# Second step of a graph layer: the rows of the second hop shifted by one product, and adjacency chunks issued among the feature reloads

## The reference

```python
R = (adj + eye) / rowsum                 # 4096 x 4096
Z = 0; Xf = X; Xa = X
for n in range(2):                       # the two steps
    A = top_p_attention(Xa, W1, W2, W3)  # softmax rows cut to the 0.9 nucleus
    Xf = R @ Xf
    Xa = A @ Xa
    Z = Z + Xf @ U1[n].T + Xa @ U2[n].T
out = layernorm(X + layernorm(X + Z))    # in outline
```

## Time and profile before

| | |
|---|---|
| time, median of 3 | 3946.87 us |
| the profiled execution's own time | 3949.58 us |
| span of the profile | 3947.7 us |
| mean granted TensorE clock | 0.978 |
| TensorE busy | 3601.9 us, 91% |
| VectorE busy | 3572.2 us, 90% |
| ScalarE busy | 3065.4 us, 78% |
| GpSimd busy | 1337.5 us, 34% |

### The profile page before, as it was taken

One profiled execution on the slowest core, in us unless ns is written; L12 is line 12 of the kernel. 1 busy time (PEld: TensorE's weight loads), 2 busy tenths in 40 slices (PEclk: granted clock), 3 DMA queues, 4 the chain that ended last, 5 costly groups with the idle time before them and its releaser, 6 DMA issues.

```text
span 3947.7 us, 66296 instructions
## 1 busy us (share of the span) xinstructions
PE 3601.9 (91%) x25368; PEld 3037.3 (77%) x25368; DVE 3572.2 (90%) x6240; ACT 3065.4 (78%) x3107; POOL 1337.5 (34%) x1508
## 2 busy tenths in 40 slices
PE   8888888888888859999999989999999999999993
PEld 5777777777777748787777768888887888888883
DVE  4999999999999969999999499999999899999994
ACT  6999999999999955555555378888888788888870
POOL 0000000000000001111111155555655569999996
PEclk9999999999999989999999999999999999999996
DMA  2112112112112140000000333333333433333331
GB/s 107 51 56 83 56 56 83 56 56 83 56 56 83 56 133 15 17 17 17 21 17 19 116 92 97 99 100 97 96 101 105 132 114 119 119 115 116 114 101 42
DMA packets 155870, 302.98 MB, mean 77 GB/s; under 512 B 16666, under 2 KB 117274, under 8 KB 151298
## 3 DMA queue, kind: packets, MB, share of 16 engines
q1 hardware_dynamic: 155522, 298.49, 23.6%
HBM read 256.67 MB, written 41.75 MB: 76 GB/s over the span
## 4 chain that ended last, share of the span: by engine, by line
DVE 50%; PE 21%; ACT 16%; POOL 7%; issue 4%; DMA 1%; DVEq 0%; SPq 0%; ACTq 0%; POOLq 0%; PEldq 0%; PEld 0%
DVE b L1344 12%; DVE b L1342 12%; PE ps L872 8%; PE ps L945 6%; DVE b L1395 4%; ACT b L1191 4%; ACT b L1192 4%; DVE b L1562 3%; DVE b L1340 3%; DVE b L1453 3%; DVE b L1451 3%; DVE b L1432 2%; POOL b L584 2%; ACT b L1172 2%; POOL b L581 2%
## 5 line engine op out<-in xcount | busy, mean ns | idle before, releaser
L872 PE MATMUL ps<-b 128*128 128x257 f32 x4096 | 911.6, 382 | 21.1 <-DMA b<-in_adjTb 11.9
L945 PE MATMUL ps<-b 128*128 128x257 f32 x4096 | 903.1, 380 | 0.0
L872 PEld LDWEIGHTS ps<-b 128*128 128x128 f32 x4096 | 776.8, 190 | 146.7 <-DMA b<-in_adjTb 13.2
L945 PEld LDWEIGHTS ps<-b 128*128 128x128 f32 x4096 | 772.0, 190 | 113.4 <-ACT b L1129 0.8
L806 PE MATMUL ps<-cb,b 128*128 128x128 f32 x4096 | 507.0, 280 | 199.6 <-ACT b L1019 161.2
L806 PEld LDWEIGHTS ps<-cb,b 128*128 128x128 f32 x4096 | 456.5, 144 | 248.7 <-ACT b L1019 184.1
L1342 DVE SCALAR_TENSOR_TENSOR b<-b 128x4096 f32<-128x4096 f32 x128 | 566.5, 4426 | 13.4 <-ACT b L1013 9.1
L1344 DVE CUSTOM_DVE_ANT_0 b<-b 128x4096 f32<-128x4096 f32 x128 | 566.4, 4425 | 4.4
L547 POOL TENSOR_TENSOR cb<-cb 128x1 f32<-128x1 f32 x32 | 39.4, 1232 | 1395.0 <-DVE cb L1324 1395.0
L1026 ACT ACTIVATE b<-ps 128x1024 f32<-128x1024 f32 x512 | 490.9, 1063 | 9.5 <-PE ps L806 9.4
L1019 ACT ACTIVATE b<-b 128x4096 f32<-128x4096 f32 x128 | 482.0, 3766 | 3.7 <-DVE b L1346 3.1
(11 more groups left out here) (194 smaller groups left out, 4899.1 us busy)
## 6 DMA issues: line engine op xcount, KB each, us to landing
b<-in_adjTb SPq DMA_DIRECT2D x256, 512.0 KB, 3.8
b<-in_adj SPq DMA_DIRECT2D x32, 2048.0 KB, 8.5
h_d<-b SPq DMA_DIRECT2D x64, 128.0 KB, 1.8
b<-h_d SPq DMA_DIRECT2D x64, 128.0 KB, 2.6
b<-in_xT SPq DMA_DIRECT2D x4, 1024.0 KB, 9.7
b<-in_xT SPq DMA_DIRECT2D x32, 128.0 KB, 8.3
gx_d<-b SPq DMA_DIRECT2D x32, 128.0 KB, 1.8
X_d<-b SPq DMA_DIRECT2D x32, 128.0 KB, 8.3
```

What stands on the lines that cost most here:

```text
L872: last = mm(b[:, 0:XA], aj[:, q % AJR, e, :], xf[:, j, :], start=(j == 0), stop=(j == NT - 1))
L945: last = mm(o[:, 0:XA], at[:, q % ATR, b, :], xa[:, j, :], start=(j == 0), stop=(j == NT - 1))
```

## The change

`rows_in(n)` takes the place of `pairs_in(n)`. Iterations 0 to 14 keep their rows 2n+2 and 2n+3. From iteration 15 on the rows are 2n+1 and 2n+2, as far as they lie in 32 to 63: iteration 15 has row 32 alone, iteration 16 has 33 and 34, ..., iteration 30 has 61 and 62, iteration 31 has row 63. `fslot` becomes {18: 0, 19: 1, ..., 31: 13, 32: 14, 34: 15}. TensorE, ScalarE, GpSimd and SyncE follow. On SyncE, chunks 3 to 6 are issued among the eight reloads, and in iteration 0 the store of rows 0 and 1 stands behind both groups of chunks.

```diff
-    fslot = {max(HT + m - RLEAD + 2, 2 * m + 4): m for m in range(HT)}
+    fslot = {max(HT + m + 2, 2 * m + 4): m for m in range(HT)}
...
-    def pairs_in(n):
...
+    def rows_in(n):
+        if n < HT - 1:
+            return [2 * n + 2, 2 * n + 3]
+        return [r for r in (2 * n + 1, 2 * n + 2) if NT <= r < 2 * NT]
...
             sp.wait_ge(g["gd"], 16 * (NT - NGX))
-            for q in range(NQ):
-                reload(q)
             sp.wait_ge(g["ks"], 16 * NT)
             sp.wait_ge(s_bar, 5 * kS[0])
...
-            ld(u2, U2T[1].rearrange("(k p) n -> p k n", p=128), s_l1)
...
+            for c in range(NCH):
+                adjchunk(AJR + c)
+                for q in range(NQ // NCH * c, NQ // NCH * (c + 1)):
+                    reload(q)
             gxload(0)
-            adjpairs(-1, 0)
+            ld(u2, U2T[1].rearrange("(k p) n -> p k n", p=128), s_l1)
             sp.wait_ge(g["xp"], 1)
             qload(1, 2)
-            adjpairs(-1, 1)
+            adjrow(-1, 1)
...
-                if HT in pairs_in(n):
+                if n == 0:
+                    adjrow(n, 0)
+                    adjrow(n, 1)
+                    rstore(n - 1)
+                elif n == HT - 1:
                     rstore(n - 1)
                     sp.wait_ge(g["ys"], 16 * NT)
                     sp.wait_ge(g["R"], NT * NCH)
                     chunked(xf, y_d)
-                adjpairs(n, 0)
-                if HT not in pairs_in(n):
+                    adjrow(n, 0)
+                else:
+                    adjrow(n, 0)
                     rstore(n - 1)
-                adjpairs(n, 1)
+                    adjrow(n, 1)
...
                     if s == 1:
-                        for p in pairs_in(n):
-                            Rmul(2 * p)
-                            if n >= 1:
+                        early = 1 <= n < NT and len(rows_in(n)) == 2
+                        for r in rows_in(n):
+                            if early and r > rows_in(n)[0]:
                                 gather_level(n)
-                            Rmul(2 * p + 1)
-                        if n == 0 or n == NT - 1:
+                            Rmul(r)
+                        if n < NT and not early:
                             gather_level(n)
```

More of the change, by code:

```diff
@@ L47, in gat_topp_kernel @@
     CT = 4
-    RLEAD = 1
     NGX = NT - 2
     KH = NT // 2
-    fslot = {max(HT + m - RLEAD + 2, 2 * m + 4): m for m in range(HT)}
+    fslot = {max(HT + m + 2, 2 * m + 4): m for m in range(HT)}
     LAST = max(fslot)
-    def pairs_in(n):
[L56 to L60, removed]
+    def rows_in(n):
+        if n < HT - 1:
+            return [2 * n + 2, 2 * n + 3]
+        return [r for r in (2 * n + 1, 2 * n + 2) if NT <= r < 2 * NT]
     ctx = ExitStack()
@@ L421, in reload @@
             def reload(q):
-                sp.wait_ge(g["av"], (NT - 1) * NCH + q // 2 + 1)
-                sp.wait_ge(g["acc"], CT * (q + 1))
+                sp.wait_ge(st[0]["av"], (NT - 1) * NCH + q // 2 + 1)
+                sp.wait_ge(st[0]["acc"], CT * (q + 1))
                 for i in range(2):
-                    sp.wait_ge(g["xd"][i], 16 * (CT // 2) * (q + 1))
+                    sp.wait_ge(st[0]["xd"][i], 16 * (CT // 2) * (q + 1))
                 ld(xa[:, CT * q:CT * (q + 1), 0:256],
@@ L478, in gxload, with adjrow @@
                         ld(gxi[:, i, :], tile_of(gx_d, 2 * p + i), g["gi"])
-            def adjpairs(n, half):
-                for p in pairs_in(n):
-                    for q in range((2 * p + half) * NCH, (2 * p + half + 1) * NCH):
+            def adjrow(n, i):
+                for r in rows_in(n)[i:i + 1]:
+                    for q in range(r * NCH, (r + 1) * NCH):
                         adjchunk(q + AJR)
             def rstore(n):
[L486 to L491, removed]
+                for r in rows_in(n):
+                    sp.wait_ge(g["yd"], r + 1)
+                    ld(tile_of(y_d if r < NT else z_d, r % NT), yr[:, r % 2, :], g["ys"])
+                if n < HT - 1:
+                    gxload(n + 2)
+            for c in range(NCH):
+                adjchunk(AJR + c)
+                for q in range(NQ // NCH * c, NQ // NCH * (c + 1)):
+                    reload(q)
             gxload(0)
-            adjpairs(-1, 0)
+            ld(u2, U2T[1].rearrange("(k p) n -> p k n", p=128), s_l1)
             sp.wait_ge(g["xp"], 1)
             qload(1, 2)
-            adjpairs(-1, 1)
+            adjrow(-1, 1)
             for n in range(LAST + 4):
@@ L619, in accumulate, with r_post @@
                     tt(hh, pzs, xa[:, t, 0:256] if s == 0 else hin, ALU.add).then_inc(g["acc"], 1)
-                def r_post(p):
-                    for i in range(2):
-                        r = 2 * p + i
+                def r_post(n):
+                    for r in rows_in(n):
+                        i = r % 2
                         po.wait_ge(g["rd"], r + 1)
@@ L626, in r_post @@
                         plink(tt(pq[:, 1, i:i + 1], prs[:, i, 256:257], mone, ALU.pow))
-                        if p >= 1:
-                            po.wait_ge(g["ys"], 32 * p)
+                        if n >= 0:
+                            po.wait_ge(g["ys"], 16 * rows_in(n)[0])
                         o = ts(yr[:, i, :], prs[:, i, 0:256], pq[:, 1, i:i + 1], 0.0, ALU.mult, ALU.add)
@@ L631, in r_post @@
                             plink(o)
-                            po.wait_ge(g["gi"], 32 * (p + 1))
+                            po.wait_ge(g["gi"], 32 * (n + 2))
                             o = tt(yr[:, i, :], yr[:, i, :], gxi[:, i, :], ALU.add)
@@ L668, in _ @@
                     if s == 1:
-                        for p in pairs_in(n - 1):
-                            r_post(p)
+                        r_post(n - 1)
                         if n - 2 in fslot:
@@ L1274, in _ @@
                     else:
-                        acts(n + 1, [2 * p + i for p in pairs_in(n) for i in range(2)], n)
+                        acts(n + 1, rows_in(n), n)
                 barrier(ac, kS[s])
```

## The result

The changed kernel takes 3954.69 us (median of 15 runs, 3952.28 to 3957.03) against 3946.87 us before (15 runs, 3944.33 to 3949.63). The ratio is 1.0018, with a 95% interval of 1.001 to 1.0026: slower by 0.18%, some 7 us. Forecast were 3952.0 us and a loss of 5.1. The interval leaves out 1, so the loss is real; but the time lies only 0.1 us under 3954.8, up to which the prediction speaks of no change. On which side of that bound it fell is luck, since runs of one kernel lie up to 5 us apart.

What follows compares the result with a forecast made beforehand. The prediction took TensorE to bound stage C's undisturbed iterations (50.61 us), VectorE having 2.4 us to spare. Its terms, -3.8 - 2.3 + 6.3 + 4.95 = +5.1 us, gave 3952.0 us on the median, range 3941 to 3958.

Steps and rivals of the forecast that it cites:

- Start of stage C: Both TensorE stalls for adjacency chunks go, 16.9 us, but only VectorE's 3.8 us wait for gather_level(0) is gained.
- starts no earlier: Start of stage C: even if Rmul(2) starts no earlier, Rmul(3) ends at 2296.9, 6 us before VectorE asks.
- Iteration 15: TensorE's wait before Rmul(32) stays; Rmul(33) leaves the stretch between gather and mask; gain 2.3 us, between 1.7 and 4.3.
- just follow: After iteration 15 VectorE keeps up: next gather 48.8 us after this one, its own loop 48.2 us.
- Rival 4: Rmul(32) really moves behind one more product, the 9.10 us wait goes too; about 3940; shares rival 2's chance, 0.15.
- Iteration 31: Rmul(63), 14.1 us, now stands ahead of gather_level(31); Tr(31) comes later; cost 6.3 us, between 0 and 10.8.
- Final pairs: GpSimd's iteration 33: final_second(13) now stands ahead of accumulate(31), on the path; cost 4.95 us, possibly 0.
- The hidden part: GpSimd's iteration 32: 16.1 us of final work ahead of scale_a(31) ends 2 us before AV(31) frees it.
- The sum: Whole kernel: -3.8 - 2.3 + 6.3 + 4.95 = +5.1 us, on the median 3952.0.
- Rival 1: GpSimd is on time in iteration 30, so iteration 31 costs 0: 3945.7 us; chance 0.15.
- Rival 2: Product loop sets stage C's pace from its start; all 16.9 us of stalls come back: 3938.9; chance 0.15, with rival 4.
- Rival 3: GpSimd comes one VectorE instruction later before zx(29) or scale_a(31), adding 4.5 us: 3956.5; chance 0.20.

Runs made afterwards that it cites:

- experiment 1: Kernel before with only the start's changes: chunks among reloads, ratio 1.0001; store of rows 0 and 1 later, 0.9994; both, 3943.61 us, 0.9988.
- Experiment 7: Changed kernel with ScalarE's evictions of AV(14) and mq(13) one search level later in iteration 15: 3955.69 us, measured once.
- Experiment 3: Changed kernel with gather_level(31) put behind the first 16 of Rmul(63)'s 64 matmuls: 3944.85 us, ratio 1.0 to the kernel before.
- experiment 5: Changed kernel without final_second of pair 13, waits and signals kept: 3950.36 us, ratio 1.0008 to the kernel before.
- Experiment 6: Changed kernel with scale_a(29) ahead of the final work in GpSimd's iteration 30: 3953.6 us, ratio 1.0017 to the kernel before.
- experiment 4: Changed kernel with gather_level(15) ahead of Rmul(32) and ScalarE's exponential of tile 17 ahead of row 32's eviction: 3941.22 us, ratio 0.9986 to before.

## Why the prediction was right

**Start of stage C.** Predicted -3.8 with Tr(0); measured -3.75 there, and 0.60 more by Tr(1), since Tr(0) took 5.60 us instead of 6.21. The 3.75 are the mechanism, found again in experiment 1; the 0.60 are luck: in the other kernels whose Tr(0) comes at 90.4 to 90.5 us its transposes took 5.9 to 6.6 us. What was not foreseen is where the removed stall of Rmul(0) went first: into logits(2), whose last quarter waits for ScalarE (5.18 us), which waits for VectorE's maximum. So Rmul(2) started only 0.3 us earlier than before in stage C's time, close to the prediction's assumption that it "starts no earlier". Chunks 4 to 6, behind the pairs of reloads, cost no wait. Chunk 7, the first behind them all, was issued at 2244.64 and awaited until 2251.84, 7.2 us later, where the median chunk of the kernel before landed 3.8 us behind its issue; that cost a bracket of 0.28 us in Rmul(1) and nothing at the end.

**Iteration 15.** Predicted -2.3 with the wait for y unchanged; measured -1.94, the wait 9.00 us, the new idle stretch 9.65 us, Tr(15) at 5.68 us. The parts: -4.30 from the gather to Tr(15), +2.03 for the slow transposes (2.0 were taken), and +0.34 ahead of the gather, where a chunk of row 32 came 0.76 us late. Experiment 7 shows the reload behind the misleading bracket. The prediction let VectorE "just follow", with gathers 48.8 us apart; that doesn't fit its own 2.0 us for slow transposes, which give 10.06 + 36.28 + 2.0 = 48.3 (36.28 from a Tr to the next gather, 2405.01 - 2368.73 in the earlier trace rows). Measured are 48.34 us, and VectorE had 0.25 us left: it held, but by less than was said. Rival 4 is out: Rmul(32) is where it was.

**Iteration 31.** Predicted +6.3, measured +7.07, the largest miss of the sum. From the gather to Tr(31) it is 6.50 us, as predicted (6.48); what was missed lies ahead of the gather: zx(29) waited 9.53 us instead of 9.25, and AV(30), slow behind it, took 16.28 instead of the 15.8 that it took before. Both count now, as VectorE's chain no longer covers them. Slow transposes in Tr(31) (5.90 against 5.39) add 0.5, which the prediction had at nothing. Experiment 3 shows the mechanism by removing it.

**Final pairs.** Predicted +4.95, measured +4.86; experiment 5 gives 4.0 to 4.3 for the whole and 5.1 counted from mq(30). The hidden part was hidden: scale_a(31) found GpSimd idle for 2.95 us, where 2 were expected.

**The sum.** -4.35 - 1.94 + 7.07 + 0.5 + 4.86 = +6.1 in stage C, against +5.1. The medians say +7.8 and the ratio's interval +4 to +10, so both fit. What of the 7.8 lies outside stage C can't be told from scatter, since runs of one kernel lie up to 5 us apart. It is in part luck that sum and forecast are only 1 us apart: the misses are -0.6, +0.4, +0.8, +0.5 and -0.1.

**The rivals.** Rival 1's condition didn't come: zx(29) waited 9.53 us. Experiment 6 brings zx(29) on time, but only by moving final work behind the scaling, which makes VectorE late instead, and gains nothing; what a GpSimd on time without that would be worth, no run shows. Rival 2 falls with experiment 1. Rival 3 needed GpSimd 4.5 us later; zx(29) waited 0.28 us longer and scale_a(31) not at all.

## What to carry to other kernels

A product can be filler or an obstacle, depending on which side of the signal it stands: behind the gather it ran for nothing beside VectorE's mask, ahead of it the same product (14.1 us) cost 7 us, all that VectorE's chain didn't cover. Where an engine must wait for data anyway (y in iteration 15), send first what another engine waits for: in experiment 4 that was worth 12.5 us. A removed stall is worth only the wait that it causes where another engine next needs this one's result, here 3.8 of 16.9 us.

## What the runs showed of the hardware

How long TensorE had been idle, between 6 and 14 us, mattered little for what followed. In the changed kernel the 32 transposes took 5.60 us behind 14.06 us of idleness, 5.68 behind 9.65 and 5.90 behind 6.12, against 3.66 at full speed; in all kernels here they took 5.3 to 6.6 us behind idle stretches of 6.1 to 14.2 us, with no order by length. Below are windows of the changed kernel around Tr(31), where TensorE was idle from 3880.13 to 3886.25. Each line gives the stretch, its length, the busy time of PE, PEld, DVE, ACT and POOL, the granted clock as a share of 2.4 GHz, the DMA share and GB/s. The clock is at 1.00 in the window from 3881, leaves the upper level in the one from 3883 (0.74 on average), stands at the lower one (0.50, 1.2 GHz) when the transposes begin, and is at 1.00 again in the window from 3891, with TensorE busy since 3886.25:

```profile
3881.00:3883.00 2.00, 0.00 (x0) 0.00 (x0) 1.29 (x1) 0.00 (x0) 1.82 (x3) 1.00 0.79 242
3883.00:3885.00 2.00, 0.00 (x0) 0.00 (x0) 2.00 (x1) 0.00 (x0) 2.00 (x1) 0.74 0.00 2
3885.00:3887.00 2.00, 0.75 (x4) 0.76 (x5) 2.00 (x4) 0.00 (x0) 1.45 (x1) 0.50 0.00 0
3887.00:3889.00 2.00, 2.00 (x11) 2.00 (x10) 0.89 (x6) 0.69 (x1) 0.99 (x3) 0.50 0.19 66
3889.00:3891.00 2.00, 2.00 (x12) 2.00 (x11) 0.00 (x0) 1.32 (x2) 1.84 (x3) 0.56 0.00 0
3891.00:3893.00 2.00, 2.00 (x17) 1.92 (x16) 0.00 (x0) 1.68 (x3) 1.77 (x4) 1.00 0.04 8
```

So making such a stretch shorter wins the time by which it is shorter, but the 1.7 to 3 us of slow transposes came back only where it went altogether, as in experiments 3 and 4, where they took 3.66 us.
